# Attention output normalised with features on partitions: values and inverses moved by DMA in place of transposes to tokens and back

## The chip, the cores and the metric

The kernel runs on 1 core of one Trainium2 chip. The metric is the device time in microseconds (us) of one execution. The median of 3 runs of the kernel before is 506.68 us (506.01 to 507.4).

## What is computed

Eight samples of 512 tokens and 256 features go through an attention layer with 16 heads of 16 features, whose output is quantised to int8 and multiplied by a quantised matrix. Cut to what matters here:

```python
q, k, v = heads(x @ wq.T * q_dc), heads(x @ wk.T * k_dc), heads(v_flat)
attn = softmax(einsum('bhqd,bhkd->bhqk', q, k) * scale)
out = einsum('bhqk,bhkd->bhqd', attn, v).transpose(0, 2, 1, 3).reshape(B, S, H)
y = einsum('bsh,oh->bso', out, w_weight) * w_dc[:, None, :] + skip
lhs_scale = max(abs(y), axis=2) / 127        # per token; rhs_scale per column of rhs
return x + int_dot(round(y / lhs_scale), round(rhs / rhs_scale)) * lhs_scale * rhs_scale
```

The softmax is left undivided until after the product with the values: the sum of the exponentials comes out of the same matmul as the values (a column of ones beside them), and its inverse is multiplied in later. That later place is what changes.

## The kernel before

**Steps and rounds.** After a prologue the kernel runs steps t = 0 to 7. Step t does the attention of sample t in 16 rounds, and beside it part A of sample t+1 (load x, modulate, normalise, q, k, v: `has_a`) and part Z of sample t-1 (from the saved attention output to the result: `has_z`). Steps 1 to 6 are three turns of a hardware loop with two steps each, so t = 3 and t = 5 begin with a jump back. Step 7 has no part A, and part Z of sample 7 follows after the last step, by code of its own.

**A round.** Round r is a group of four heads (r // 4) and a tile of 128 keys (r % 4). On PE it is four matmuls for the scores (L933), eight small ones for the values of round r-1 (L946, into `o_acc`, where each head has 32 partitions: 16 of values, then the sum), and then the fill of that round, if it has one. ACT takes the exponentials of the scores in two pieces (L479) and after each fourth round saves `o_acc` into `o_t[:, g, :]` (`save_o`, L465). The last group of sample t-1 is saved in round 0 of step t. Scores of round r+1 need the exponentials of round r, through two buffers.

**Fills.** Part Z of sample t-1 in PE's rounds: `to_natural` (rounds 1 and 2, four times four transposes, from features on partitions to tokens on partitions), `to_features` (round 3, eight transposes back), `projected` with w (rounds 5 and 6, L1078), the transposes of the quantised rows and the integer product (rounds 14 and 15). Part A: `x_transposed` (round 4), then q, k, the skip matrix, and v (rounds 7 to 13, L969, L978, L990). PE runs its program in this order, so a fill that has to wait holds up the scores behind it.

**DVE** does in a step with both parts, in this order: `modulate` and `measure` of x, `z_normalise` (for each 128 tokens the reciprocal of the sums, L742, and the product, L743), `normalise_x` (which waits for a power taken by POOL, L385), `z_features` (two copies from PSUM, L750), two `split`s of the transposed x (L519 to L521), `z_quantise`, and then part A.

**DMA.** SP's queue carries nearly all transfers, issued in program order: after the six transfers to `k_stack` that end a step (L310) it loads x, the style row and three more rows for the next sample (L249, L250, L253), then x once more for the residual (L289), then the 24 transfers of q and k parts.

PSUM tiles for fills come from three banks of `work` in turn; `work_freed` and `work_ready` count them.

Of the kernel before, what the change touches and what calls it, by code (L numbers as in the profile page):

```python
# [19 lines left out]
F32 = mybir.dt.float32  # L20
# [7 lines left out]
P = 128  # L28
# [30 lines left out]
def adaln_ffn_kernel(nc, x, cond, wq, wk, wv, ww, wu, rhs, out):  # L59
# [12 lines left out]
    SETUP_USES, ROW_USES, RHS_USES, A_USES, Z_USES = 7, 2, 3, 12, 12  # L72
# [5 lines left out]
    no_shift_dram = nc.dram_tensor("no_shift_dram", (3, NH, S), BF16).ap()  # L78
    rows_dram = nc.dram_tensor("rows_dram", (B, 3, H), F32).ap()

    ctx = ExitStack()
    with ctx:
# [54 lines left out]
        shift_rest = sb("shift_rest", [NH, S])  # L137
# [17 lines left out]
        inv_den = sb("inv_den", [P, KT, NH])  # L155
        o_nat = sb("o_nat", [P, KT, H])
# [36 lines left out]
        st_ready, exp_done, pv_done, o_saved = sem("st_ready"), sem("exp_done"), sem("pv_done"), sem("o_saved")  # L193
        on_ready, ot_ready, yq_ready, yqt_ready = sem("on_ready"), sem("ot_ready"), sem("yq_ready"), sem("yqt_ready")
# [5 lines left out]
        FULL = ([("on", q) for q in range(KT)] + [("ot", i) for i in range(2)] + [("xt", c) for c in range(HC)]  # L200
# [46 lines left out]
        def _(sp):  # L247
# [26 lines left out]

            def step(t, par, has_a, has_z, base, bank, prologue=False):
# [162 lines left out]
        def _(act):  # L438
# [23 lines left out]
            def save_o(t, g):  # L462

                act.wait_ge(pv_done, t * ROUNDS + KT * (g + 1))
                nc.scalar.activation(o_t[:, g, :], o_acc[:, :], ACT.Copy).then_inc(o_saved, 1)  # L465

            def step(t, par, has_a, has_z, base, bank, prologue=False):
# [5 lines left out]
                for r in range(ROUNDS):  # L473
# [7 lines left out]
                    if r % KT == 0 and r > 0:  # L481
                        save_o(t, r // KT - 1)
# [18 lines left out]
        def _(dve):  # L501
# [111 lines left out]
            def step(t, par, has_a, has_z, base, bank, prologue=False):  # L613
# [41 lines left out]
                if has_z:  # L655
                    z_quantise(ready, pz)
# [91 lines left out]
            def z_features(ready):  # L748
                for i in range(2):
                    link(nc.vector.tensor_copy(o_t2[:, :, 2 * i * P:2 * (i + 1) * P],  # L750
                                               ready("ot", i).rearrange("p (c t) -> p c t", c=HC)))
                    dve.sem_inc(ot_ready, 1)
                    dve.sem_inc(work_freed, 1)
# [394 lines left out]
```

## Time and profile before

| | before |
|---|---|
| median of 3 runs | 506.68 us (506.01 to 507.4) |
| span of the profiled execution | 505.8 us |
| PE busy | 469.7 us, 93% |
| DVE busy | 274.6 us, 54% |
| ACT busy | 290.4 us, 57% |
| POOL busy | 117.2 us, 23% |
| mean granted clock of TensorE | 0.953 |
| DMA, SP's queue | 39.75 MB, 46.8% of 16 engines' span |

The profiled execution is read from its first to its last instruction (the span); the median of the runs lies 0.9 us above it. Busy shares are means over a prologue, eight steps and an end that have different limits. A granted clock of 1 is TensorE's upper level (2.4 GHz), 0.5 its lower one (1.2 GHz). Rows of a timeline merge instructions of one line that follow one another: "x8" is eight of them, the second number is how long the eight took together, and brackets hold the idle time of that engine ahead of the row and what ended it.

### The profile page before, as it was taken

What the parts mean: (1) busy time and instruction counts of PE and PEld (TensorE: products, weight loads), DVE (VectorE), ACT (ScalarE), POOL (GpSimd) and SP (SyncE); (2) the same over time, 40 slices, a digit from 0 to 9 for tenths busy, and PEclk for the clock granted to TensorE, in tenths of its full rate; (3) what the DMA queues carried; (4) which work ended last, traced back from release to release, by engine and by line L of the source; (5) the groups of instructions that cost most, each with busy time, mean ns of one, the idle gap of its engine ahead of it and who ended that gap; (6) DMA issues with size and microseconds to landing.
All of it is one profiled execution on the core that took longest, in us unless ns stands there. A gap on an engine that the chain in (4) does not pass through costs nothing.

```text
span 505.8 us, 8873 instructions
## 1 busy us (share of the span) xinstructions
PE 469.7 (93%) x2626; PEld 225.0 (44%) x2626; DVE 274.6 (54%) x653; ACT 290.4 (57%) x333; POOL 117.2 (23%) x123
## 2 busy tenths in 40 slices
PE   5877999999999999699999999789999999999983
PEld 5753245344553545334543445325454444533251
DVE  4875634267536754357445755447544764444055
ACT  4032675665657575366657665456756665577920
POOL 8532113020324022220322223130232214020021
PEclk9587899999999999889999999979999999999997
DMA  6075629620967068720788049620597219520021
GB/s 202 0 164 112 96 49 129 121 84 2 135 98 191 1 87 102 159 80 1 107 101 191 27 60 127 149 92 0 82 108 152 84 35 128 93 84 1 1 85 41
DMA packets 42029, 45.04 MB, mean 89 GB/s; under 512 B 3896, under 2 KB 39992, under 8 KB 41944
## 3 DMA queue, kind: packets, MB, share of 16 engines
q1 hardware_dynamic: 40096, 39.75, 46.8%
q0 software_dynamic: 1040, 3.72, 1.9%
q8 instruction: 32, 0.52, 0.5%
q10 hardware_dynamic: 832, 0.80, 0.5%
q14 instruction: 29, 0.24, 0.2%
HBM read 14.83 MB, written 4.27 MB: 38 GB/s over the span
## 4 chain that ended last, share of the span: by engine, by line
PE 82%; ACT 4%; issue 4%; DVE 4%; DMA 3%; SPq 1%; POOL 1%; POOLq 0%; ACTq 0%; DVEq 0%
PE o_acc L946 22%; PE scores L933 20%; PE work L969 9%; PE work L990 9%; PE work L809 8%; PE work L1078 6%; ACT probs L479 4%; PE work L978 3%; PE work L838 2%; DMA q_stack<-in_L_cond_w_weight_dram 1%; PE work L1092 1%; DMA rows<-in_cond_dram 1%; SPq L310 1%; DMA q_stack<-no_shift_dram 1%; ACT o_t L465 0%
## 5 line engine op out<-in xcount | busy, mean ns | idle before, releaser
L479 ACT ACTIVATE probs<-scores 128x1024 f32<-128x1024 f32 x256 | 248.0, 1024 | 133.4 <-PE scores L933 133.4
L933 PE MATMUL scores<-q_stack,k_stack 99*128 99x512 bf16 x512 | 138.8, 390 | 13.6 <-issue 9.0
L946 PE MATMUL o_acc<-probs,v_aug 128*32 128x512 f32 x1024 | 139.4, 617 | 0.0
L406 POOL TENSOR_TENSOR parts<-rest,parts 128x512 bf16<-128x512 f32 x32 | 40.8, 1276 | 200.1 <-DVE parts L678 200.1
L933 PEld LDWEIGHTS scores<-q_stack,k_stack 99*128 99x128 bf16 x512 | 43.8, 99 | 85.7 <-ACT probs L479 29.4
L990 PE MATMUL work<-vs_w,x_t 128*128 128x512 f32 x192 | 53.4, 423 | 2.7 <-DVEq L668 2.7
L969 PE MATMUL work<-x_t,qk_w 128*128 128x512 f32 x192 | 53.5, 415 | 0.0
L425 POOL TENSOR_TENSOR rest<-rest,x_res 128x512 f32<-128x512 f32 x16 | 20.0, 1270 | 131.0 <-DVEq L793 131.0
L990 PEld LDWEIGHTS work<-vs_w,x_t 128*128 128x128 f32 x192 | 35.8, 197 | 26.9 <-issue 13.6
L946 PEld LDWEIGHTS o_acc<-probs,v_aug 128*32 128x32 f32 x1024 | 20.4, 109 | 55.8 <-issue 54.1
L969 PEld LDWEIGHTS work<-x_t,qk_w 128*128 128x128 f32 x192 | 34.6, 189 | 23.9 <-DVEq L677 11.7
L1078 PE MATMUL work<-w_demod,o_t 128*128 128x256 f32 x128 | 31.5, 390 | 0.0
L1078 PEld LDWEIGHTS work<-w_demod,o_t 128*128 128x128 f32 x128 | 23.1, 190 | 14.3 <-DVEq L646 5.0
L519 DVE TENSOR_SCALAR upper<-work 128x512 int32<-128x512 int32 x24 | 16.5, 689 | 18.9 <-PE work L978 9.9
L627 DVE TENSOR_TENSOR v_aug<-work,rows 128x256 f32<-128x256 f32 x32 | 13.6, 424 | 24.3 <-PE work L990 24.1
L675 DVE SCALAR_TENSOR_TENSOR rest<-work,col_now,parts 128x512 f32<-128x512 f32 x16 | 12.0, 750 | 25.2 <-ACT parts L459 23.2
L776 DVE TENSOR_SCALAR y_qt<-work 128x512 bf16<-128x512 f32 x14 | 9.7, 692 | 27.9 <-PE work L809 25.8
L459 ACT ACTIVATE parts<-work,col_now 128x512 bf16<-128x512 f32 x16 | 11.0, 688 | 23.6 <-PE work L969 23.6
L459 ACT ACTIVATE parts<-work 128x512 bf16<-128x512 f32 x16 | 9.6, 598 | 24.9 <-PE work L969 24.9
L809 PE MATMUL work<-ident,o_nat 128*128 128x128 f32 x128 | 18.6, 282 | 4.0 <-DVE o_nat L771 2.4
L809 PEld LDWEIGHTS work<-ident,o_nat 128*128 128x128 f32 x128 | 13.6, 140 | 17.6 <-issue 5.9
L465 ACT ACTIVATE o_t<-o_acc 128x512 f32<-128x512 f32 x32 | 19.3, 604 | 3.0 <-PE o_acc L946 3.0
(108 smaller groups left out, 430.2 us busy)
## 6 DMA issues: line engine op xcount, KB each, us to landing
q_stack<-parts SPq DMA_DIRECT2D x96, 128.0 KB, 5.2
k_stack<-parts SPq DMA_DIRECT2D x96, 128.0 KB, 5.3
x_sb<-in_x_dram SPq DMA_DIRECT2D x8, 512.0 KB, 5.5
x_res<-in_x_dram SPq DMA_DIRECT2D x8, 512.0 KB, 3.9
out_dram<-rest POOLq DMA_DIRECT2D x7, 512.0 KB, 4.7
rows<-rows_dram SPq DMA_DIRECT2D x8, 384.0 KB, 5.5
rows<-in_cond_dram SPq DMA_DIRECT2D x8, 128.0 KB, 5.4
out_dram<-rest SPq DMA_DIRECT2D x2, 256.0 KB, 2.1
```

Of the source, the lines that this page charges most:

```text
L406: nc.gpsimd.tensor_tensor(parts[:, n, 2, :], rest[:, n, :], parts[:, n, 1, :], ALU.subtract).then_inc(low_ready, 1)
L425: nc.gpsimd.tensor_tensor(res[:, two, :], res[:, two, :], x_res[:, two, :], ALU.add).then_inc(res_added, 1)
L459: nc.scalar.activation(parts[:, n, 0, :], work[:, (bank + use) % NW, :], ACT.Copy, scale=scale).then_inc(hi_ready, 1)
L465: nc.scalar.activation(o_t[:, g, :], o_acc[:, :], ACT.Copy).then_inc(o_saved, 1)
L479: nc.scalar.activation(probs[:, r % 2, pair:pair + 2, :], scores[:, pair:pair + 2, :], ACT.Exp).then_inc(exp_done, 1)
L519: link(nc.vector.tensor_scalar(top.bitcast(I32), value.bitcast(I32), UPPER_BITS, None, ALU.bitwise_and))
L809: return nc.tensor.transpose(dst, src, ident[0:rows, 0:rows])
L933: last = nc.tensor.matmul(scores[:, j, :], k_stack[0:ROWS, par, h, kt * P:(kt + 1) * P], q_stack[0:ROWS, par, h, :], start=True, stop=True)
L946: last = nc.tensor.matmul(o_acc[DV * j:DV * (j + 1), :], v_aug[:, par, kt, 4 * g + j, :], probs[:, r % 2, j, :], start=(kt == 0), stop=(kt ...
L969: last = nc.tensor.matmul(bank, lhs, right, start=(n == 0), stop=(n == len(operands) - 1))
L990: last = nc.tensor.matmul(bank, lhs, right, start=(n == 0), stop=(n == len(operands) - 1))
L1078: last = nc.tensor.matmul(bank[:, k * H:(k + 1) * H], lhs, right, start=(n == 0), stop=(n == len(operands) - 1))
```

## The change

The 24 transposes of `to_natural` and `to_features` and all of `z_normalise` and `z_features` go, for the samples 0 to 6. Instead SP moves, for each of the four groups of heads, the sums (four partitions of `o_t`, into 16 rows of a new tile `den`) and the values (four transfers of 16 partitions each, straight into `o_t2`, which has features on partitions): 20 transfers in a step. DVE takes one reciprocal of `den`, SP stores it to a tensor in DRAM, waits until it is there, and loads it back in two transfers, each sum repeated over the 16 features of its head (`inv_t`, which lies over half of `rest`). DVE then multiplies `o_t2` by `inv_t` in two halves (`z_scale`), and each half releases one `projected`. ACT's first save in a step waits until the values and sums of the sample before are moved. The end of the last sample is as before.

```diff
-    SETUP_USES, ROW_USES, RHS_USES, A_USES, Z_USES = 7, 2, 3, 12, 12
+    SETUP_USES, ROW_USES, RHS_USES, A_USES, Z_USES = 7, 2, 3, 12, 6
+            def attention_out(g):
+
+                sp.dma_start(den[g * 4 * KT:(g + 1) * 4 * KT, :], o_t[D:P:DV, g, :]).then_inc(den_loaded, 16)
+                half_of = (g % 2) * (P // 2)
+                for j in range(4):
+                    sp.dma_start(o_t2[half_of + j * D:half_of + (j + 1) * D, g // 2, :],
+                                 o_t[j * DV:j * DV + D, g, :]).then_inc(val_loaded, 16)
...
                 if has_z:
                     z = t - 1
+                    for g in range(G):
+                        wait(o_saved, z * G + (g + 1))
+                        attention_out(g)
+                    wait(den_ready, z + 1)
+                    sp.dma_start(inv_dram.rearrange("h (k t) -> (h k) t", k=KT), den_inv[:, :]).then_inc(inv_stored, 16)
+                    wait(inv_stored, z * 16 + 16)
+                    for c in range(HC):
+                        sp.dma_start(inv_t[:, c, :], inv_dram[c * HG:(c + 1) * HG, :].unsqueeze(1)
+                                     .broadcast_to([HG, D, S])).then_inc(inv_loaded, 16)
                     wait(res_added, z * 2 + 2)
...
+                if g == 0 and later:
+                    act.wait_ge(val_loaded, t * G * 4 * 16)
+                    act.wait_ge(den_loaded, t * G * 16)
                 nc.scalar.activation(o_t[:, g, :], o_acc[:, :], ACT.Copy).then_inc(o_saved, 1)
...
-                if has_z:
-                    z_normalise(ready)
                 if has_a and not prologue:
                     normalise_x(a)
                 if has_z:
-                    z_features(ready)
+                    z_inverses(t - 1)
                 if has_a:
                     for c in range(HC):
                         split(x_t[:, 0, c, :], x_t[:, 1, c, :], ready("xt", c))
...
                 if has_z:
+                    z_scale(t - 1)
                     z_quantise(ready, pz)
...
+            def z_inverses(z):
+                dve.wait_ge(den_loaded, z * G * 16 + G * 16)
+                nc.vector.reciprocal(den_inv[:, :], den[:, :]).then_inc(den_ready, 1)
+
+            def z_scale(z):
+                dve.wait_ge(val_loaded, z * G * 4 * 16 + G * 4 * 16)
+                dve.wait_ge(inv_loaded, z * HC * 16 + HC * 16)
                 for i in range(2):
...
+                    two = slice(2 * i * P, 2 * (i + 1) * P)
+                    nc.vector.tensor_tensor(o_t2[:, :, two], o_t2[:, :, two], inv_t[:, :, two], ALU.mult
+                                            ).then_inc(ot_ready, 1)
...
-                return {1: lambda: [to_natural(0), to_natural(1)], 2: lambda: [to_natural(2), to_natural(3)],
-                        3: lambda: [to_features(0), to_features(1)], 5: lambda: projected(0), 6: lambda: projected(1),
+                _, _, projected, quantised_transposed, int_product = z_stages(z, pz, claimed)
+                return {5: lambda: projected(0), 6: lambda: projected(1),
```

DVE, in the loop, from the end of `measure` to the start of `z_quantise`; before (`L621` and `L508` rows are register work for the waits; "waits" names the semaphores):

```order
L539 TENSOR_SCALAR var_eps<-mv 128x4 [waits dve_step]
L742 RECIPROCAL inv_den<-work 128x16 [waits work_ready]
L743 TENSOR_TENSOR o_nat<-work,inv_den 128x256 [waits dve_step]
L544 TENSOR_SCALAR x_sb<-x_sb,mv,rstd 128x256 [waits rstd_ready]
L750 COPY o_t<-work 128x2x256 [waits work_ready]
L519 TENSOR_SCALAR upper<-work 128x512 [waits work_ready]
L520 CAST x_t<-upper 128x512 [waits dve_step]
L521 TENSOR_TENSOR x_t<-work,upper 128x512
L759 TENSOR_TENSOR o_nat<-work,skip 128x512 [waits work_ready]
```

And the same place in the changed kernel:

```order
L567 TENSOR_SCALAR var_eps<-mv 128x4 [waits dve_step]
L572 TENSOR_SCALAR x_sb<-x_sb,mv,rstd 128x256 [waits rstd_ready]
L777 RECIPROCAL den_inv<-den 64x128 [waits den_loaded]
L547 TENSOR_SCALAR upper<-work 128x512 [waits work_ready]
L548 CAST x_t<-upper 128x512 [waits dve_step]
L549 TENSOR_TENSOR x_t<-work,upper 128x512
L781 ISA [waits val_loaded]
L784 TENSOR_TENSOR o_t<-o_t,rest 128x2x256 [waits inv_loaded]
L791 TENSOR_TENSOR o_nat<-work,skip 128x512 [waits work_ready]
```

(The tile `o_t2` shows as `o_t` and `inv_t` as `rest`.) The copies that released `projected` stood ahead of the two splits; the products that release it now stand behind them. The reciprocal stands ahead of the splits and waits for a transfer.

SP, in the loop, between the loads for the next sample and the first part of q; before:

```order
L249 DMA x_sb<-in_x_dram 128x4x256
L250 DMA rows<-in_cond_dram 128x256
L253 DMA rows<-rows_dram 128x768
L289 ISA [waits res_added]
L289 DMA x_res<-in_x_dram 128x4x256
L310 DMA q_stack<-parts 16x8x512 [waits hi_ready]
```

And in the changed kernel:

```order
L261 DMA rows<-rows_dram 128x768
L285 DMA den<-o_t 16x1x128 [waits o_saved]
L288 DMA o_t<-o_t 16x512 x4
L308 DMA inv_dram<-den_inv 64x128 [waits den_ready]
L311 DMA rest<-inv_dram 128x1x512 [waits inv_stored]
L311 DMA rest<-inv_dram 128x1x512
L314 ISA [waits res_added]
L314 DMA x_res<-in_x_dram 128x4x256
L335 DMA q_stack<-parts 16x8x512 [waits hi_ready]
```

The pair L285 and L288 stands there four times, once for each group: 20 transfers, and behind them one store and two loads, each with a wait, on the one queue.

## Rows read from the trace of the kernel before

**Rows 1.** The page, part 4: the chain that ended last, by engine.
```profile
PE 82%; ACT 4%; issue 4%; DVE 4%; DMA 3%; SPq 1%; POOL 1%; POOLq 0%; ACTq 0%; DVEq 0%
```

**Rows 2.** Timeline of PE, step t=4: start us, us, engine, line, op.
```profile
271.05 1.03 PE L933 MATMUL scores<-q_stack,k_stack 99*128 99x512 bf16 x4
...
284.08 1.09 PE L809 MATMUL work<-ident,x_sb 128*128 128x128 f32 x8
285.01 1.03 PE L933 MATMUL scores<-q_stack,k_stack 99*128 99x512 bf16 x4
...
286.96 2.00 PE L1078 MATMUL work<-w_demod,o_t 128*128 128x256 f32 x8
```

**Rows 3.** Timeline of PE, step t=7: starts of rounds 7 and 11, none between filled.
```profile
464.94 1.27 PE L933 MATMUL scores<-q_stack,k_stack 99*128 99x512 bf16 x4
...
473.40 1.28 PE L933 MATMUL scores<-q_stack,k_stack 99*128 99x512 bf16 x4
```

**Rows 4.** Timeline of DVE, step t=4.
```profile
281.77 1.38 DVE L544 TENSOR_SCALAR x_sb<-x_sb,mv,rstd 128x256 f32<-128x256 f32 x4 [0.32 <-DVE o_nat L743]
...
285.06 0.69 DVE L519 TENSOR_SCALAR upper<-work 128x512 int32<-128x512 int32 x1 [0.31 <-DVE o_t L750]
...
289.21 0.69 DVE L759 TENSOR_TENSOR o_nat<-work,skip 128x512 f32<-128x512 f32 x1 [0.32 <-PE work L1078]
```

**Rows 5.** Timeline of POOL, step t=4.
```profile
277.78 1.04 POOL L385 TENSOR_TENSOR rstd<-var_eps,half 128x4 f32<-128x4 f32 x1 [1.77 <-DVE var_eps L539]
```

**Rows 6.** Groups by line and form: count, busy us, mean ns.
```profile
L527 DVE TENSOR_TENSOR x_sb<-x_sb,rows 128x1024 f32<-128x1024 f32 x8 | 10.0, 1253 | 19.3 <-DMA rows<-in_cond_dram 11.8 <-issue 7.0 <-DVE skip L629 0.2
...
L742 DVE RECIPROCAL inv_den<-work 128x16 f32<-128x16 f32 x32 | 8.3, 258 | 18.8 <-PE work L809 12.7 <-DVE o_nat L743 6.1
...
L611 DVE RECIPROCAL demod<-demod 128x80 f32<-128x80 f32 x1 | 0.7, 653 | 0.5 <-ACT demod L448 0.5
```

**Rows 7.** Timeline of SP's queue, end of step t=3 and start of t=4.
```profile
263.26 3.87 SPq L310 DMA_DIRECT2D k_stack<-parts  x6
...
269.04 0.34 SPq L253 DMA_DIRECT2D rows<-rows_dram  x1
```

**Rows 8.** Line L310: one issue, ns min/median/max, of SP's queue.
```profile
L310 SPq DMA_DIRECT2D q_stack<-parts x96: 547/588/1457, 29.6 to 425.8; - x96
```

**Rows 9.** Timeline of SP's queue, prologue: a store, and the load that waits for it.
```profile
26.25 0.37 SPq L263 DMA_DIRECT2D rows_dram<-o_nat  x1
28.02 0.37 SPq L253 DMA_DIRECT2D rows<-rows_dram  x1
```

**Rows 10.** Line L289, the load of 512 KB to x_res, last line of the view.
```profile
DMA to landing us min/median/max: 3.4/3.9/6.2
```

**Rows 11.** Line L253, the broadcast load of 384 KB, last line.
```profile
DMA to landing us min/median/max: 4.6/5.5/6.1
```

**Rows 12.** Timeline of PE after two long idle stretches.
```profile
46.99 1.04 PE L933 MATMUL scores<-q_stack,k_stack 99*128 99x512 bf16 x4 [2.45 <-DMA q_stack<-no_shift_dram]
...
214.28 1.89 PE L933 MATMUL scores<-q_stack,k_stack 99*128 99x512 bf16 x4 [4.36 <-issue]
```

**Rows 13.** Windows: PE busy, then granted clock, DMA share and GB/s.
```profile
49.00:50.00 1.00, 1.00 (x3) 0.50 1.09 155
...
211.00:213.00 2.00, 0.00 (x0) 0.80 0.93 314
...
219.00:221.00 2.00, 2.00 (x15) 0.99 0.02 6
```

**Rows 14.** Timeline of SP's queue, step t=1.
```profile
98.77 0.33 SPq L253 DMA_DIRECT2D rows<-rows_dram  x1
```

**Rows 15.** Timeline of PE, step t=1.
```profile
115.63 1.99 PE L1078 MATMUL work<-w_demod,o_t 128*128 128x256 f32 x8
```

**Rows 16.** Timeline of SP's queue, step t=3.
```profile
209.61 0.34 SPq L253 DMA_DIRECT2D rows<-rows_dram  x1
```

**Rows 17.** Timeline of PE, step t=3.
```profile
231.97 1.99 PE L1078 MATMUL work<-w_demod,o_t 128*128 128x256 f32 x8
```

More of the change, by code:

```diff
@@ L78, in adaln_ffn_kernel @@
     no_shift_dram = nc.dram_tensor("no_shift_dram", (3, NH, S), BF16).ap()
+    inv_dram = nc.dram_tensor("inv_dram", (NH, S), F32).ap()
     rows_dram = nc.dram_tensor("rows_dram", (B, 3, H), F32).ap()
@@ L136, in adaln_ffn_kernel @@
         shift = sb("shift", [NH, 3, S], BF16)
-        shift_rest = sb("shift_rest", [NH, S])
+        shift_rest = upper[0:NH, :]
         probs = sb("probs", [P, 2, 4, S])
@@ L155, in adaln_ffn_kernel @@
         inv_den = sb("inv_den", [P, KT, NH])
+        den = sb("den", [NH * KT, P])
+        den_inv = sb("den_inv", [NH * KT, P])
+        inv_t = rest[:, 0:2, :]
         o_nat = sb("o_nat", [P, KT, H])
@@ L193, in adaln_ffn_kernel @@
         st_ready, exp_done, pv_done, o_saved = sem("st_ready"), sem("exp_done"), sem("pv_done"), sem("o_saved")
+        val_loaded, den_loaded, inv_loaded = sem("val_loaded"), sem("den_loaded"), sem("inv_loaded")
+        den_ready, inv_stored = sem("den_ready"), sem("inv_stored")
         on_ready, ot_ready, yq_ready, yqt_ready = sem("on_ready"), sem("ot_ready"), sem("yq_ready"), sem("yqt_ready")
@@ L197, in adaln_ffn_kernel @@
         spare = sem("spare")
-        FULL = ([("on", q) for q in range(KT)] + [("ot", i) for i in range(2)] + [("xt", c) for c in range(HC)]
+        FULL = ([("xt", c) for c in range(HC)]
                 + [("rows", n) for n in range(ROW_USES)] + [("rhs", n) for n in range(RHS_USES)]
@@ L460, in high_part, with save_o @@
                                      scale=scale).then_inc(hi_ready, 1)
-            def save_o(t, g):
+            def save_o(t, g, later=True):
                 act.wait_ge(pv_done, t * ROUNDS + KT * (g + 1))
+                if g == 0 and later:
+                    act.wait_ge(val_loaded, t * G * 4 * 16)
+                    act.wait_ge(den_loaded, t * G * 16)
                 nc.scalar.activation(o_t[:, g, :], o_acc[:, :], ACT.Copy).then_inc(o_saved, 1)
@@ L481, in step @@
                     if r % KT == 0 and r > 0:
-                        save_o(t, r // KT - 1)
+                        save_o(t, r // KT - 1, has_z)
                     if r == 0 and has_z:
@@ L1041, in z_fills @@
             def z_fills(z, pz, claimed):
-                to_natural, to_features, projected, quantised_transposed, int_product = z_stages(z, pz, claimed)
-                return {1: lambda: [to_natural(0), to_natural(1)], 2: lambda: [to_natural(2), to_natural(3)],
-                        3: lambda: [to_features(0), to_features(1)], 5: lambda: projected(0), 6: lambda: projected(1),
+                _, _, projected, quantised_transposed, int_product = z_stages(z, pz, claimed)
+                return {5: lambda: projected(0), 6: lambda: projected(1),
                         14: lambda: [quantised_transposed(0), quantised_transposed(1)],
@@ L1106, in last_claimed @@
                 elif kind == "on":
[L1107 removed]
+                    pe.wait_ge(on_ready, n - NW + 1)
                 return work[:, use % NW, :]
@@ L1120, in _ @@
                 int_product(i)
-DVE_LINKS = 80
+DVE_LINKS = 60
 _INS = ['x', 'cond_2048', 'L0_cond_q_weight', 'L0_cond_k_weight', 'L0_cond_v_weight', 'L0_cond_w_weight',
```

8 lines of the change are left out of this document (1 added, 7 removed).

## The prediction

> **What bounds the kernel now.** I read the chain first: 82% of it is PE [rows 1], so work taken off PE can pay. But the share is a mean over rounds of two kinds, so I read one step of the loop, t=4, in PE's timeline [rows 2]. Round 0 starts at 271.05, the transposes of x (round 4) at 284.08, round 5 at 285.01, and its fill, the first `projected`, at 286.96. I call this last start P0, since everything behind it keeps its distance from it. Four rounds and the scores and values of the fifth take 284.08 - 271.05 = 13.03 us. What they would take without fills is seen in step 7, whose rounds 7 to 10 have none: 473.40 - 464.94 = 8.46 us for four [rows 3]. This is the pace at which PE and ACT feed each other. So removing the fills of rounds 1 to 3 can give about 2.6 us a step: x_transposed would start at 271.05 + 8.46 + 1.96 (scores and values as in round 5, 286.96 - 285.01) = 281.5. Over seven steps that is 18 us, and the question is whether P0 follows.
>
> **P0 does not follow: DVE's order.** In the trace `projected` is released by the copies ahead of the splits. In the new order the product stands behind both splits, and they need the transposed x. The two splits take 289.21 - 285.06 = 4.15 us [rows 4]. The first bank of x is full about half-way through the eight transposes (1.09 us), so the splits run from 281.5 + 0.7 = 282.2 to 286.35. The product has 512 elements per partition from SBUF; L527 does 1,024 in 1.25 us [rows 6], hence 0.65. With 0.1 for the signal, P0 is 287.1: 0.2 us later than before, and PE, which is ready for it at 281.5 + 2.88 = 284.4, stands still for 2.7 us. This floor holds even if every transfer is free. The 2.6 us won ahead are spent waiting. PE's removed time is real, but it is given back three rounds later.
>
> **The transfers, in a step inside a turn (t = 2, 4, 6).** SP's queue is busy with `k_stack` until 267.13 and ends the issue of its next loads at 269.38 [rows 7]. Then come 20 issues in a row. No SP issue of this size from SBUF to SBUF with few rows is in the trace. The nearest are L310's, also SBUF to SBUF: 0.547 us at the shortest, 0.588 in the median [rows 8], and 3.87 us for six, 0.65 each with the queue full [rows 7]. From DRAM or to it one takes 0.34 to 0.37 [rows 7, 9]. I take 0.60 (bounds 0.40 and 0.65). The sixteenth, which carries the last sums, is issued at 269.38 + 15 x 0.60 = 278.4. It lands within 1.8: the store of 24 KB and the load that waits for it start 1.77 us apart [rows 9]. That makes 280.2. DVE's `normalise_x` no longer waits for the four pairs ahead of it but only for POOL's power, which ends at 278.82 [rows 5]; with its 1.38 us [rows 4] DVE is free at 280.3. The reciprocal has 128 elements per partition; 16 take 0.258 us and 80 take 0.653 [rows 6], so by that slope 0.95: 281.25. SP has meanwhile issued the last four value transfers, until 281.4. Its store and wait take 1.77: 283.2. The two broadcast loads carry 512 KB together. The load of 512 KB at L289 lands in 3.9 (3.4 at best) [rows 10]; the broadcast load of 384 KB takes 4.6 at best and 5.5 in the median [rows 11], behind other loads. I take 4.6, since here the queue ahead is empty but there are two of them: 287.8. The product adds 0.65 and the signal 0.1: P0 = 288.55, 1.6 us later than before, and PE waits 4.1 us. The ends: 0.40 an issue, with loads of 3.4, gives 281.25 + 1.77 + 3.4 + 0.75 = 287.2 (the floor, +0.2); 0.65 an issue, with loads of 6.1, gives an SP free at 269.38 + 13.0 = 282.4 and P0 = 291.0 (+4.1).
>
> **The other steps.** At t=1 SP has its rows issued at 99.1 [rows 14]. So 99.1 + 12.0 = 111.1 for the twentieth issue (the reciprocal is done at 110.85), then 1.77 + 4.6 + 0.75 = 118.25 against 115.63 [rows 15]: +2.6 (bounds 0 and +5.1). At t = 3 and 5 the jump back of the loop delays PE but not SP: SP is through at 209.95 [rows 16], the same sum gives loads landed at 209.95 + 12.05 + 1.77 + 4.6 = 228.4. P0 stood at 231.97 [rows 17]. The transposes of x move from 229.1 to 226.5, the splits end at 231.35, P0 is 232.1: the floor rules, +0.2 each. Step 7 has no splits, but its SP queue is as late after `k_stack`; I price it as an inner step, +1.6. Waits alone: 2.6 + 3 x 1.6 + 2 x 0.2 + 1.6 = +9.4 us (floor everywhere +1.4; upper ends 5.1 + 12.3 + 0.4 + 4.1 = +22).
>
> The Trainium skill (DMA: Bandwidth & Descriptors, Issuing engines are not separate DMA queues) says that initiating a DMA is usually small beside the DMA itself. Row and rule differ here: L310's issue is 0.55 us or more [rows 8]. By the rule the sums at t=1 would be there before DVE asks, and that step would cost about 1.3 us less.
>
> **The clock.** The new stalls of PE are 2.7 us (t = 3, 5), about 4 (t = 2, 4, 6, 7) and longer at t=1. What such stalls do is in the trace. After 4.36 us of waiting at the jump the four scores took 1.89 us instead of 1.03 [rows 2, 12]; the granted clock had fallen before 213 and was back at about 219 [rows 13]. After 2.45 us at 46.99 the scores were still fast, and two microseconds on the clock stood at 0.50 [rows 12, 13]. So half clock lasts some 7 us, of which about 2 lie in the stall, and in the other 5 PE loses (1.89 - 1.03)/1.89 = 0.45 of its time: 2.3 us. It falls into the rounds with the largest fills, where PE sets the pace and nothing covers it. Five stalls of about 4 us and more, and one of the two short ones: 6 x 2.3 = +13.8 us.
>
> **Costed at nothing.** ACT's first save now waits for the last value transfer, issued at 281.4 and landed at 283.2; ACT is there at about 282. Behind it stand the exponentials of round 5, and PE's values of round 4 need the save; both are done by 286, while PE waits for P0 until 288.55. Without that cover it would cost 1.2 us a step. DVE's removed work is ahead of the splits and gives DVE nothing it could use, since the splits wait for PE. The x_res load comes later, and its reader, POOL's addition, comes at the step's end. The extra 1.1 MB a step (512 KB of values, 512 KB of broadcast inverses, 64 KB beside them) fall between 270 and 288, behind the x loads and ahead of the parts of q. Banks of `work` come free earlier than before.
>
> **The sum.** 9.4 + 13.8 = 23.2 on a span of 505.8, which lies 0.9 below the median of the runs: 529.9, I say 530 us.
>
> **The rivals.**
> (a) The clock holds. The stalls are there, but split so that the clock does not fall. For it: PE works densely ahead of the stall, unlike at 46.99. Against it: both stretches in [rows 12] were followed by a fall. 505.8 + 0.9 + 9.4 = 516.
> (b) The broadcast loads are slower than I take. They read 8 rows of DRAM, each repeated 16 times. If each runs on half of the engines, the moving part of 3.9 - 1.8 = 2.1 us doubles: +2.1 a step where the transfers are last (t = 1, 2, 4, 6, 7), +10.5 in all, 540. At t = 3 and 5 there are 2.9 us of slack, which cover it. No row here has such an outer count of 8, so the trace neither supports nor excludes it. The Trainium skill speaks for it (DMA: Bandwidth & Descriptors, Why a DMA increments its semaphore by 16 and not by 1): the number of engines is the largest up to 16 that divides the slowest dimensions of both access patterns, which would be 8.
> (c) No change: issues at 0.40, loads at 3.4, and a clock that holds. Every step is at the floor: 506.7 + 1.4 = 508.
> (d) Faster. If rounds 0 to 3 ran at PE's own pace of 1.96 a round instead of 2.115, T would be 0.6 earlier, and P0 0.4 us earlier than before in each step; with transfers at their low ends and no clock fall, 7 x 0.4 = 2.8 us: 504. The full 18 us (488) need the product ahead of the splits or splits that are off the path; the order on DVE speaks against that. The point from which it turns is P0 before 286.96.
>
> **How the numbers follow.** Chances: my forecast (stalls and clock) 0.47, own range 521 to 538; (b) 0.23; (a) 0.15; (c) 0.07, of which 0.06 within 0.3%; (d) 0.08. A measurement of this kernel tells about 0.3% (1.5 us) from no change. Faster 0.08, same 0.06, slower 0.86. The range leaves out (d) and most of (c) below and the upper tail of (b) above, and takes in +22 us of waits with seven clock falls (545): 509 to 545.
>
> **What would show it.** Right: PE rounds 0 to 3 start about 2.1 us apart; PE idles ahead of L1109 (projected) in each step by 2.7 us or more, released by DVE's L784; L784 itself idles on the landing of L311 in t = 1, 2, 4, 6; SP's twenty issues take about 12 us; the granted clock shows 0.5 behind the stalls, and the mean clock falls from 0.953 to below 0.92. Wrong: issues of 0.3 us (then the floor holds in inner steps), L784 idle only behind the splits, a mean clock near 0.95 (then about 516), or DVE waiting for `den` so long that the splits start late (then above 540).

## The result and the profile after

The changed kernel takes 560.12 us (median of 4 runs, 555.54 to 560.98), the kernel before 506.35 us (505.92 to 507.4) on the same chip. The ratio is 1.1035, with a 95% interval of 1.0983 to 1.1086: 53.8 us slower, where +23 was forecast and 545 us was the upper end. The profiled execution has a span of 559.3 us against 505.8, and a mean granted clock of 0.921 against 0.953. Runs over 1.5% above the fastest of their kernel are left out of all comparisons, which touches only two runs of the first kernel with later projections.

The page of the changed kernel: the engines' busy time, the bytes of SP's queue (q1), and the chain that ended last, by engine (compare [rows 1]) and by line of code.

```profile
PE 468.7 (84%) x2458; PEld 214.8 (38%) x2458; DVE 263.5 (47%) x604; ACT 290.4 (52%) x333; POOL 118.3 (21%) x123
...
q1 hardware_dynamic: 46704, 47.56, 46.4%
...
PE 47%; SPq 26%; DMA 11%; DVE 6%; issue 6%; ACT 3%; DVEq 0%; POOLq 0%; POOL 0%; ACTq 0%
SPq L288 13%; PE o_acc L978 11%; PE scores L965 10%; PE work L1001 8%; PE work L1109 7%; DMA rest<-inv_dram 7%; SPq L335 5%; PE work L1022 5%; SPq L285 3%; PE work L1010 2%; DMA inv_dram<-den_inv 2%; ACT probs L507 2%; PE work L870 1%; PE work L841 1%; DMA q_stack<-in_L_cond_w_weight_dram 1%
```

PE was 82% of the chain and is 47%. SP's queue (SPq) has taken a quarter of it, and the largest single line of the chain is L288, the issue of the value transfers. PE's busy time hardly fell (468.7 from 469.7 us) although 168 transposes are gone: the matmuls of `projected` were busy for 44.0 us in place of 31.5 and the scores for 143.6 in place of 138.8, since a part of them ran at half clock. The view of waits (who waited <- for whom: us in all, times, longest) names the new stalls:

```profile
PE work L1109 <- DVE o_t L784: 41.2, 7, 7.4
DVE o_t L784 <- DMA rest<-inv_dram: 35.2, 7, 9.3
DVE den_inv L777 <- DMA den<-o_t: 22.0, 7, 7.5
...
ACT o_t L493 <- DMA o_t<-o_t: 17.5, 6, 5.0
PE o_acc L978 <- ACT o_t L493: 13.8, 5, 3.7
```

Now step t=4. First PE's timeline, which answers to [rows 2]:

```profile
292.89 1.03 PE L965 MATMUL scores<-q_stack,k_stack 99*128 99x512 bf16 x4
...
303.71 1.09 PE L841 MATMUL work<-ident,x_sb 128*128 128x128 f32 x8
...
308.62 1.07 PE L978 MATMUL o_acc<-probs,v_aug 128*32 128x512 f32 x8 [2.95 <-ACT o_t L493]
315.85 3.77 PE L1109 MATMUL work<-w_demod,o_t 128*128 128x256 f32 x8 [6.17 <-DVE o_t L784]
319.42 1.84 PE L965 MATMUL scores<-q_stack,k_stack 99*128 99x512 bf16 x4
```

The transposes of x start 10.82 us after round 0 (13.03 before): the gain of the freed rounds is there. P0 stands 22.96 us after round 0, and stood 15.91 after it. SP's queue in the same step, which answers to [rows 7, 9]:

```profile
292.26 1.06 SPq L285 DMA_DIRECT2D den<-o_t  x1
293.37 2.49 SPq L288 DMA_DIRECT2D o_t<-o_t  x4
...
296.70 3.36 SPq L288 DMA_DIRECT2D o_t<-o_t  x4
...
303.47 0.59 SPq L285 DMA_DIRECT2D den<-o_t  x1
304.10 2.41 SPq L288 DMA_DIRECT2D o_t<-o_t  x4
306.65 0.50 SPq L308 DMA_DIRECT2D inv_dram<-den_inv  x1
308.56 1.35 SPq L311 DMA_DIRECT2D rest<-inv_dram  x2
```

And DVE's, which answers to [rows 4]:

```profile
300.69 1.60 DVE L572 TENSOR_SCALAR x_sb<-x_sb,mv,rstd 128x256 f32<-128x256 f32 x4 [1.17 <-POOL rstd L410]
305.25 0.94 DVE L777 RECIPROCAL den_inv<-den 64x128 f32<-64x128 f32 x1 [2.95 <-DMA den<-o_t]
...
309.19 0.68 DVE L549 TENSOR_TENSOR x_t<-work,upper 128x512 fp32r<-128x512 f32 x1
315.03 1.29 DVE L784 TENSOR_TENSOR o_t<-o_t,rest 128x512 f32<-128x512 f32 x2 [5.15 <-DMA rest<-inv_dram]
```

Read together they give the chain. The fourth transfer of sums is issued at 303.47, because fifteen issues stand ahead of it. It lands, and the reciprocal runs from 305.25 to 306.19. SP is busy with the last four values until 306.51 and then stores. The loads follow at 308.56, and the product at 315.03, long after the splits (end 309.87). At t=3, an odd step, the product waits for the loads too:

```profile
250.80 1.29 DVE L784 TENSOR_TENSOR o_t<-o_t,rest 128x512 f32<-128x512 f32 x2 [2.68 <-DMA rest<-inv_dram]
```

The clock in the stall, by windows (busy us of PE, PEld, DVE, ACT and POOL; the last three are granted clock, DMA share and GB/s):

```profile
308.00:310.00 2.00, 1.07 (x8) 0.16 (x8) 1.72 (x3) 2.00 (x3) 0.00 (x0) 1.00 0.02 5
310.00:312.00 2.00, 0.00 (x0) 0.00 (x0) 0.00 (x0) 0.40 (x1) 0.00 (x0) 0.70 0.51 165
312.00:314.00 2.00, 0.00 (x0) 0.00 (x0) 0.00 (x0) 0.00 (x0) 0.00 (x0) 0.50 1.01 217
...
318.00:320.00 2.00, 2.00 (x6) 1.18 (x6) 0.34 (x1) 0.00 (x0) 0.00 (x0) 0.50 0.00 0
320.00:322.00 2.00, 2.00 (x12) 0.31 (x9) 1.74 (x6) 1.40 (x2) 0.00 (x0) 0.74 0.00 0
```

PE falls to its lower level while it stands still and keeps it behind the stall (by an estimate from the windows' clocks, from 310.8 to 321): the eight matmuls of `projected` take 3.77 us and not 2.00.

The whole difference can be split at P0. From the starts of round 0 and P0 in both timelines, P0 comes later after round 0 by 6.2 (t=1, counted from the span's start), 6.0, 2.3, 7.0, 2.5, 8.3 and 5.7 us (t = 2 to 7): 38.1 us in all. From P0 to the next round 0 (in t=7 to the end) the steps are longer by 2.2, 3.0, 2.2, 2.1, 2.0, 1.8 and 2.2: 15.4 us. Together that is the 53.5 us between the spans. In all seven steps it is the product L784 that releases P0, and the loads L311 that release L784.

### The profile page after: what moved, and what is told of

Read it like the earlier page. It is cut to its first block, busy times and chain, and to the rows that moved or that the text cites. A ratio compares the mean times of both kernels' runs of the same rounds, so it can differ in the third digit from the quotient of the medians.

```text
span 559.3 us, 8531 instructions
## 1 busy us (share of the span) xinstructions
PE 468.7 (84%) x2458; PEld 214.8 (38%) x2458; DVE 263.5 (47%) x604; ACT 290.4 (52%) x333; POOL 118.3 (21%) x123
## 4 chain that ended last, share of the span: by engine, by line
PE 47%; SPq 26%; DMA 11%; DVE 6%; issue 6%; ACT 3%; DVEq 0%; POOLq 0%; POOL 0%; ACTq 0%
SPq L288 13%; PE o_acc L978 11%; PE scores L965 10%; PE work L1001 8%; PE work L1109 7%; DMA rest<-inv_dram 7%; SPq L335 5%; PE work L1022 5%; SPq L285 3%; PE work L1010 2%; DMA inv_dram<-den_inv 2%; ACT probs L507 2%; PE work L870 1%; PE work L841 1%; DMA q_stack<-in_L_cond_w_weight_dram 1%
## 5 line engine op out<-in xcount | busy, mean ns | idle before, releaser
L965 PE MATMUL scores<-q_stack,k_stack 99*128 99x512 bf16 x512 | 143.6, 396 | 14.7 <-issue 8.5
L978 PE MATMUL o_acc<-probs,v_aug 128*32 128x512 f32 x1024 | 139.5, 617 | 13.8 <-ACT o_t L493 13.8
L965 PEld LDWEIGHTS scores<-q_stack,k_stack 99*128 99x128 bf16 x512 | 41.7, 101 | 110.5 <-ACT probs L507 57.6
L1109 PE MATMUL work<-w_demod,o_t 128*128 128x256 f32 x128 | 44.0, 504 | 41.2 <-DVE o_t L784 41.2
L1022 PE MATMUL work<-vs_w,x_t 128*128 128x512 f32 x192 | 52.1, 415 | 2.7 <-DVEq L695 2.7
L1109 PEld LDWEIGHTS work<-w_demod,o_t 128*128 128x128 f32 x128 | 30.7, 251 | 59.0 <-issue 46.3
L493 ACT ACTIVATE o_t<-o_acc 128x512 f32<-128x512 f32 x32 | 19.3, 604 | 21.8 <-DMA o_t<-o_t 17.5
L791 DVE TENSOR_TENSOR o_nat<-work,skip 128x512 f32<-128x512 f32 x16 | 11.1, 691 | 34.2 <-PE work L1109 34.2
L784 DVE TENSOR_TENSOR o_t<-o_t,rest 128x512 f32<-128x512 f32 x14 | 9.1, 688 | 35.2 <-DMA rest<-inv_dram 35.2
L484 ACT ACTIVATE parts<-work 128x512 bf16<-128x512 f32 x16 | 9.6, 598 | 24.2 <-PE work L1001 24.2
```

What stands on the lines that cost most here:

```text
L484: nc.scalar.activation(parts[:, n, 0, :], work[:, (bank + use) % NW, :], ACT.Copy, scale=scale).then_inc(hi_ready, 1)
L965: last = nc.tensor.matmul(scores[:, j, :], k_stack[0:ROWS, par, h, kt * P:(kt + 1) * P], q_stack[0:ROWS, par, h, :], start=True, stop=True)
L978: last = nc.tensor.matmul(o_acc[DV * j:DV * (j + 1), :], v_aug[:, par, kt, 4 * g + j, :], probs[:, r % 2, j, :], start=(kt == 0), stop=(kt ...
L1022: last = nc.tensor.matmul(bank, lhs, right, start=(n == 0), stop=(n == len(operands) - 1))
L1109: last = nc.tensor.matmul(bank[:, k * H:(k + 1) * H], lhs, right, start=(n == 0), stop=(n == len(operands) - 1))
```

## The experiments

Each edits the changed kernel. Ratios are to the kernel before on the same chip, with 95% intervals.

**No inverse.** The reciprocal, the transfers of sums, the store and the loads go, so the division is left out; the product becomes a maximum of `o_t2` with itself, in the same place:

```diff
-                sp.dma_start(den[g * 4 * KT:(g + 1) * 4 * KT, :], o_t[D:P:DV, g, :]).then_inc(den_loaded, 16)
...
-                    sp.dma_start(inv_dram.rearrange("h (k t) -> (h k) t", k=KT), den_inv[:, :]).then_inc(inv_stored, 16)
...
-                    z_inverses(t - 1)
...
-                    nc.vector.tensor_tensor(o_t2[:, :, two], o_t2[:, :, two], inv_t[:, :, two], ALU.mult
+                    nc.vector.tensor_tensor(o_t2[:, :, two], o_t2[:, :, two], o_t2[:, :, two], ALU.max
```

> The changed kernel without its inverse chain: no transfers of sums, no reciprocal, no store to DRAM, no broadcast loads; the product keeps its place behind the splits, with another operand that is there already (the division by the sums is left out). My theory (transfers of the inverse set the start of the first projection, and DVE's order is the next limit): the first projection starts at the floor, about 16.1 us after round 0 (22.96 now, 15.9 before), PE still idles some 2.7 us ahead of it, and the time is 508 to 520 us, by how often the clock falls. Rival (DVE's order is no limit): the projection starts when PE comes to it, 13.4 us after round 0, and the time is about 488.

Measured: 513.3 us, 1.0133 (1.0113 to 1.0153), clock 0.958. PE's timeline in t=4:

```profile
292.57 1.99 PE L1098 MATMUL work<-w_demod,o_t 128*128 128x256 f32 x8 [2.13 <-DVE o_t L773]
```

P0 stands 16.5 us after round 0 in t = 2, 4 and 6 and 17.6 to 18.8 in t = 3 and 5. With nothing but the order on DVE left, PE still waits about 2 us a step, and the kernel is no faster than before. So the floor is real, and of the 54 us about 46 hang on the inverse.

**No inverse, product ahead of the splits.** The same, and `z_scale` moves to where `z_inverses` stood:

```diff
-                    z_inverses(t - 1)
+                    z_scale(t - 1)
...
-                    z_scale(t - 1)
```

> As e1_no_inverse (the division is left out), and the product stands ahead of the two splits on DVE. My theory: it is then bound only by the landing of the 16 value transfers, some 12 us after round 0, PE idles 0 to 1 us ahead of the first projection, the clock stays up, and the saving of the transposes shows: 490 to 496 us. Rival (the value transfers alone are as slow as the whole): above 505.

Measured: 494.36 us, 0.9757 (0.9734 to 0.9779). P0 comes 14.5 us after round 0 in t = 2 and 4. Moving the product by one place on DVE is worth 19 us. The freed rounds pay when nothing stands between them and P0, but only 12 us, and in a kernel that leaves out the division.

**The order of the broadcast load.** The 16 copies become the outermost dimension. The bytes are the same, but the features get the inverse of another head:

```diff
-                        sp.dma_start(inv_t[:, c, :], inv_dram[c * HG:(c + 1) * HG, :].unsqueeze(1)
-                                     .broadcast_to([HG, D, S])).then_inc(inv_loaded, 16)
+                        sp.dma_start(inv_t[:, c, :], inv_dram[c * HG:(c + 1) * HG, :].unsqueeze(0)
+                                     .broadcast_to([D, HG, S])).then_inc(inv_loaded, 16)
```

> The changed kernel with the two broadcast loads read in another order: 16 copies outermost, 8 heads inside, in place of 8 heads outermost (same bytes, same 2 KB pieces; features get the inverse of another head, so part of the result is not the reference's). If the loads run on half of the engines because of the outer count of 8: they land in about 4.3 us instead of 6.4, the first projection is 2.1 us earlier in each of seven steps, and the time falls by about 15 us to 545. If the 6.4 us are the price of a broadcast from DRAM behind other transfers: no change, 560.

Measured: 547.36 us, 1.0839 (1.0768 to 1.0909). SP's queue and DVE in t=4:

```profile
302.10 1.21 SPq L311 DMA_DIRECT2D rest<-inv_dram  x2
...
306.78 1.29 DVE L784 TENSOR_TENSOR o_t<-o_t,rest 128x512 f32<-128x512 f32 x2 [3.36 <-DMA rest<-inv_dram]
```

From the issue of the loads to the product it takes 4.7 us, and 6.5 in the changed kernel; over the steps t = 2 to 7 it is 4.3 to 4.9 us, and 5.4 to 7.7 in the changed kernel. The windows show why. In the changed kernel, before the load of x_res joins:

```profile
311.00:311.50 0.50, 0.00 (x0) 0.00 (x0) 0.00 (x0) 0.00 (x0) 0.00 (x0) 0.50 0.51 150
311.50:312.00 0.50, 0.00 (x0) 0.00 (x0) 0.00 (x0) 0.00 (x0) 0.00 (x0) 0.50 0.52 143
```

And with the copies outermost:

```profile
304.00:304.50 0.50, 0.00 (x0) 0.00 (x0) 0.00 (x0) 0.00 (x0) 0.00 (x0) 0.50 0.83 324
304.50:305.00 0.50, 0.00 (x0) 0.00 (x0) 0.00 (x0) 0.00 (x0) 0.00 (x0) 0.50 1.10 303
```

The load with 8 outer rows keeps a share of 0.51 to 0.52 of the 16 engines busy at about 150 GB/s, the one with 16 outer copies 0.83 and more at over 300. This is rival (b), and it is real. The rule of the Trainium skill that I weighed for it (DMA: Bandwidth & Descriptors, Why a DMA increments its semaphore by 16 and not by 1) gives 8 engines and 16 for these two shapes. The trace agrees, with a share of 0.51 against 0.83 and more. The run is 12.8 us faster than the changed kernel by the medians and 10 us by the ratios; some 15 us were expected.

**Work for PE in the stall.** Dummy matmuls into the claimed bank ahead of the wait for the product, 44 of them, and in a second kernel 20:

```diff
+                    if i == 0 and pad:
+                        for _ in range(pad):
+                            nc.tensor.matmul(bank[:, 0:P], ones[:, :], ident[:, :], start=True, stop=True)
```

> The changed kernel with 44 matmuls that feed nothing ahead of PE's wait for the first projection, about 5 us of work inside the stall. My theory (the stall costs the clock too, about 2.5 us a step): the first projection starts at the same distance from round 0, its eight matmuls take 2.0 us instead of 3.8, the granted clock stays near 1 and the time falls by 12 to 18 us, to 542 to 548. Rival (the clock falls for other reasons, or costs nothing, since PE has slack): 560, or above it if the padding delays something.

> As e4_keep_clock with 20 matmuls in place of 44. There each took 0.23 us (two passes of 0.115), so the padding lasted 10 us, longer than the stall; 20 take 4.6 us, less than the stall of 5 to 7. My theory (the stall costs the clock as well): first projection at the same distance from round 0 as in the changed kernel, its eight matmuls in 2.0 us and not 3.8, mean clock 0.95 or more, 542 to 548 us. Rival (the clock is not what the stall costs): 558 to 562.

Measured: with 44, 579.65 us, 1.1429 (1.1385 to 1.1473), a miss. PE's timeline at t=3:

```profile
251.56 10.09 PE L1104 MATMUL work<-ident,ones 128*128 128x128 f32 x88
```

The trace counts two instructions for each f32 matmul, and the padding took 10.1 us, longer than the stall that it should fill. With 20: 546.72 us, 1.0809 (1.075 to 1.0868), clock 0.945. Its PE timeline at t=4:

```profile
302.39 1.07 PE L978 MATMUL o_acc<-probs,v_aug 128*32 128x512 f32 x8 [2.85 <-ACT o_t L493]
303.39 6.34 PE L1104 MATMUL work<-ident,ones 128*128 128x128 f32 x40
309.57 1.89 PE L1112 MATMUL work<-w_demod,o_t 128*128 128x256 f32 x8
```

P0 stands 22.8 us after round 0, as late as without the padding, but `projected` takes 1.89 us. The 40 instructions took 6.34 us, 0.16 each, where those of the longer padding took 0.115: the clock had fallen here too, and came back while the padding ran. The windows of this run at t=4 show it (granted clock third from the end):

```profile
303.00:304.00 1.00, 1.00 (x11) 0.61 (x4) 0.66 (x2) 1.00 (x2) 0.00 (x0) 0.69 0.17 35
305.00:306.00 1.00, 1.00 (x7) 1.00 (x6) 0.00 (x0) 0.00 (x0) 0.00 (x0) 0.50 0.61 195
307.00:308.00 1.00, 1.00 (x11) 1.00 (x10) 0.50 (x1) 0.00 (x0) 0.00 (x0) 1.00 1.02 331
```

So at t=4 (and at t=2) the half clock fell on matmuls that feed nothing, behind PE's wait for ACT of 2.85 us; at t=3 the clock stood at 1.00 throughout. Behind P0, the steps t = 1 to 6 are together 0.4 us longer than before, and 13.2 us longer in the changed kernel, while P0 comes as late as there (0.6 us earlier over all seven steps together). So the surplus behind P0 is the clock, and 13.4 us of the median (11 by the ratios) is its price.

**Sums first.** SP issues three transfers of sums ahead of the values and the store ahead of the last four:

```diff
-                    for g in range(G):
+                    for g in range(G - 1):
                         wait(o_saved, z * G + (g + 1))
-                        attention_out(g)
+                        sums_out(g)
+                    attention_out(0)
+                    wait(o_saved, z * G + G)
+                    sums_out(G - 1)
+                    attention_out(1)
+                    attention_out(2)
...
+                    attention_out(3)
```

> The changed kernel with SP's issues in another order: the four transfers of sums ahead of most values, the store after the values of three groups, the last four values while the store is under way. If SP's queue of twenty issues of 0.7 us sets when the inverse starts: the store goes out 3 us earlier, the first projection comes about 19.7 us after round 0 in place of 23.0, and the time is 535 to 543 us. Rival (the loads or DVE's place set it, and the order does not matter): 555 to 560.

Measured: 557.9 us, 1.1006 (1.0939 to 1.1074): a miss, no clear change. SP's queue, first at t=3, then at t=4:

```profile
227.57 2.54 SPq L289 DMA_DIRECT2D o_t<-o_t  x4
233.90 0.59 SPq L284 DMA_DIRECT2D den<-o_t  x1
234.53 5.60 SPq L289 DMA_DIRECT2D o_t<-o_t  x8
...
303.68 0.50 SPq L314 DMA_DIRECT2D inv_dram<-den_inv  x1
304.23 2.49 SPq L289 DMA_DIRECT2D o_t<-o_t  x4
306.92 1.35 SPq L318 DMA_DIRECT2D rest<-inv_dram  x2
```

At t=4, counted from round 0, the store comes 2.7 us earlier, but the four value issues behind it end only 3.0 us after it was issued (a store and the load behind it were 1.9 apart): the loads gain 1.4 us and P0 1.5. At t=3 SP stands still from 230.1 to 233.9, since the save of the last group only comes in round 0, which the jump back delays; P0 is 1.5 us later there. Over the whole kernel this order, with the number of issues as it was, made no clear difference.

**Projections later.** `projected` moves from rounds 5 and 6 to rounds 8 and 9, and DVE's product behind its share of k; the inverse lies in the other half of `rest`, and its loads wait for POOL's store out of it. The second kernel has sums first and a semaphore for each group too; the third is the second with the product one place earlier on DVE:

```diff
+                    late = [fills.pop(5), fills.pop(6)] if has_z else None
...
+                        fills[8] = lambda: [k0(), late[0]()]
+                        fills[9] = lambda: [late[1](), q1()]
```

> The changed kernel, transfers untouched, with both projections (and DVE's product and quantising) moved behind q and k of the first group: rounds 8 and 9 in place of 5 and 6; the inverse lies in the other half of rest. My theory (the chain of transfers is only too long for round 5, about 23 us after round 0; round 8 ends its own work at about 22): PE's stall at the projection falls under 2 us, ACT's wait for the values stays at some 3 us a step and is now the largest loss, and the time is 500 to 515 us. Rival (the transfers cost by contention with the parts of q and k, or by the clock): above 530.

> e6 and e7 together, and a semaphore for each group of heads, so that ACT's first save waits for the first group's values alone. My theory: no stall of PE over 1 us is left in a step but the jump of the loop, rounds 0 to 6 run at 2.1 us, the clock stays near 0.96 to 1, and the time is 486 to 494 us, faster than both kernels. Rival (what was taken off PE comes back in any order, in the rounds of part A, where DVE now has the quantising between the parts of q and k): 500 to 508.

> e8_late_sums_groups with DVE's product by the inverse ahead of the second part of A (k of the first group) and no longer behind it. In e8 PE stood still for 4 us at the projection while DVE did that part, although the inverse had landed. My theory: P0 follows the matmuls of k without a stall over 1 us, the clock stays up outside the loop's jumps, and the time is 495 to 508 us. Rival (something else than DVE's place holds the projection, or the parts of q and k are late in turn): above 525.

Measured: 554.45 us, the median of the two runs that count (560.09 over all four), 1.0952 (1.0857 to 1.1048); 543.88 us, 1.0742 (1.0687 to 1.0796); 511.99 us, 1.0131 (1.0055 to 1.0208). The first two are misses by 40 and 50 us, and the third lies 4 us above what was expected. DVE's timeline of the second at t=4:

```profile
303.43 0.75 DVE L714 SCALAR_TENSOR_TENSOR rest<-work,col_now,parts 128x512 f32<-128x512 f32 x1 [5.17 <-ACT parts L493]
...
306.66 0.69 DVE L711 TENSOR_TENSOR rest<-work,parts 128x512 f32<-128x512 f32 x1 [1.56 <-ACT parts L493]
...
308.18 2.24 DVE L798 TENSOR_TENSOR o_t<-o_t,rest 128x512 f32<-128x512 f32 x2
```

The product does not wait for a DMA any more (no bracket): it waits for its turn behind work that waits for ACT, and PE's `projected` waits 3.96 us for it, in each of the steps t = 1 to 6 and in the first kernel too. I had moved PE's side and left the same mistake on DVE. In the third kernel this is mended, in PE's timeline at t=4:

```profile
290.35 1.99 PE L1129 MATMUL work<-w_demod,o_t 128*128 128x256 f32 x8 [0.81 <-DVE o_t L799]
...
321.84 0.61 PE L1143 MATMUL work<-rhs_q,y_qt 128*128 128x256 bf16 x4 [1.72 <-DVEq L827]
```

In t = 1 to 6 the stall is down to 0.8 us and the half clock is gone; of the 54 us about 46 come back, 31 of them by this one place on DVE. It is still 1.3% slower than the kernel before. Two remainders are seen: the integer product now waits for DVE's queue (5.5 us in three waits), and in t=7 the projection still starts late and at half clock (3.78 us). The first comes with the semaphores: the three kernels that have one for each group show this wait (4.9 to 6.4 us), and none of the others does. How the rest divides was not measured; the two products together also take 2.24 us in the second kernel, and 1.29 in the changed one.

**A semaphore for each group.** ACT's save waits for its own group's transfers, not for all:

```diff
-                if g == 0 and later:
-                    act.wait_ge(val_loaded, t * G * 4 * 16)
-                    act.wait_ge(den_loaded, t * G * 16)
+                if later:
+                    act.wait_ge(val_loaded[g], t * 4 * 16)
+                    act.wait_ge(den_loaded[g], t * 16)
```

> The changed kernel with only the semaphores split by group of heads, so that ACT's save in round 4 waits for the first group's transfers and no longer for all twenty. My theory, as in the prediction (that wait is covered by the longer wait for the inverse): PE's stall of some 3 us ahead of its values in round 5 goes, its stall ahead of the projection grows by as much, and the time stays, 555 to 562 us. Rival (the wait of ACT costs on its own): 6 steps x 3 us less, about 541.

Measured: 559.59 us, 1.1055 (1.0971 to 1.114). ACT's wait (17.5 us) and PE's for ACT (13.8) are gone from the view, and PE's wait for the product has grown by 4.8 us, from 41.2:

```profile
PE work L1112 <- DVE o_t L787: 46.0, 7, 10.1
...
PE work L1126 <- DVEq L815: 4.9, 3, 1.9
```

The time is the same, but not all of PE's 13.8 us went into the wait for the product. P0 stands 7.3 us earlier after round 0 over all steps together, and the stretches behind P0 are 6.4 us longer, in t = 2, 4 and 6 above all, where PE waits for DVE's queue ahead of the integer product. Why the extra semaphores bring that wait was not examined. So the run bounds the price of ACT's wait at some 7 us, and does not show it to be nothing.

**The values left out**, alone, and with the other order of the load. With the values goes ACT's wait for them:

```diff
-                for j in range(4):
-                    sp.dma_start(o_t2[half_of + j * D:half_of + (j + 1) * D, g // 2, :],
-                                 o_t[j * DV:j * DV + D, g, :]).then_inc(val_loaded, 16)
```

> This kernel is the changed one without its sixteen value transfers a step; the tile of the values is set to zero once and the values stay left out. The four transfers of sums, the reciprocal, the store, the two loads and the product stand where they stood. Theory (SP's queue of issues delays the inverse): the fourth transfer of sums no longer stands behind twelve value transfers, so in an even step the reciprocal waits for normalise_x alone (done about 9.4 us after the start of round 0), then 0.95 + 1.9 for the store and its wait and 6.5 from the issue of the loads to the product: the first projected starts 18.5 to 19.5 us after round 0 in even steps instead of 22.96 at t=4 (15.9 before), and the save of ACT waits for nothing. The time is 532 to 545 us, and DVE's wait for the inverse falls from 35 to 13 to 20 us. Rival (the issues lie beside other work, and only the round trip of the inverse counts): less than 5 us come back, 555 to 560.

> This kernel is the one without value transfers, and its two loads of the inverse have the 16 copies as their outermost dimension, as in the run with that order, so the features get the inverses of another head; the values are left out. Theory (both delays lie in one chain and add up): loads to product 4.7 us instead of 6.5, the first projected 16.8 to 17.6 us after round 0 in even steps, which is close to the floor set by the splits (16.5); DVE's wait for the inverse below 8 us in all, the clock falls in fewer steps, time 515 to 530 us. Rival (with the values gone the load's order is hidden anyway): no more than 3 us below the kernel without value transfers.

Measured: 538.6 us, 1.0648 (1.0567 to 1.0729), and 524.16 us, 1.0348 (1.0273 to 1.0423). SP's queue of the first at t=4:

```profile
281.36 3.80 SPq L285 DMA_DIRECT2D den<-o_t  x4
292.37 0.50 SPq L304 DMA_DIRECT2D inv_dram<-den_inv  x1
```

The sums are out long before DVE asks. P0 stands 18.5 to 20.2 us after round 0 in even steps (21.9 to 24.2 in the changed kernel; 18.5 to 19.5 expected), in the second kernel 17.7 to 18.0, which is 0.1 to 0.4 over what was expected. Both medians lie in their ranges, but DVE's wait for the inverse fell from 35.2 only to 22.9 us (13 to 20 expected) and to 14.3 (below 8 expected). By the ratios some 20 us hang on the sixteen value transfers (21.5 by the medians). How much of that is ACT's wait was not separated. With them gone the order of the load is worth 15 us (14.4 by the medians): the two delays lie in one chain and add up.

## Why the prediction was off

The direction and the place (PE ahead of `projected`, released by L784) were as forecast, and in the even steps the mechanism too (L784 waits for L311). In the odd steps DVE's order was forecast to rule, and the chain of transfers ruled there as well. The size was wrong: P0 came 38.1 us later in all, and the forecast gave it 9.4, with 22 as the upper end. What failed is the length of the chain of transfers, in two of its terms: the price of an issue on SP and the time of the broadcast loads. Step by step:

- **The freed rounds.** Forecast: x's transposes 10.4 us after round 0. Measured 10.82 at t=4. Right.
- **The floor by DVE's order.** Forecast 0.2 us over the old P0. Without the inverse P0 is 0.6 us over it in t=2 and t=4. Right as a floor, but it rules nowhere in the changed kernel.
- **The issues on SP: the term that was mis-sized most.** I took 0.60 us an issue, bounds 0.40 and 0.65, from [rows 7, 8]. Fifteen issues took 11.2 us at t=4 (0.75 each, from 292.26 to 303.47) and 12.7 at t=3 (0.84 each); all twenty took 14.25 at t=4, where 12.0 was forecast. A single value issue is 0.52 at best and 0.59 in the median, but some take up to 1.78. At t=4 the long ones are in the first two groups (1.06 for the first issue, 3.36 for four of the second group, 2.41 for four of the last). [rows 7] had shown 0.65 for L310 in a full queue, and I used this as an upper bound, not as the likely value; even the bound was too low. SP also came to them 0.8 us later after round 0 than before. Together the store is issued 3.4 us later against round 0 than forecast.
- **The reciprocal and the round trip of the store.** Forecast 0.95 and 1.77; measured 0.94 and 1.91. Right.
- **The broadcast loads.** Forecast 4.6 us, measured 6.47 at t=4 (5.4 to 7.7 over the steps), and 4.7 with the copies outermost (4.3 to 4.9). My term was right for 16 engines, and the case was rival (b), whose price was right (2.1 against 1.8) and whose chance was 0.23. I had called the rows silent on it, and the Trainium skill's rule, which the prediction cites, was the only evidence there was. It deserved more.
- **The odd steps.** Forecast: the floor, +0.2, because SP is not held up by the jump. Measured +2.3 and +2.5, and at t=3 too the product waits for the loads. SP did start 4.4 us ahead of round 0 at t=3, as forecast (4.3), but its fifteen issues took 12.7 us in place of 9.0 and the loads 5.7 in place of 4.6. The slack of 2.9 us that I had counted was gone.
- **t=4 as a sum.** 17.5 (forecast P0 after round 0) + 3.4 (issues and start) + 0.14 (store) + 1.87 (loads) + 0.07 = 23.0, against 22.96 measured.
- **The clock.** Forecast 13.8 us, as six falls of 2.3; 15.4 us lie behind P0, as seven of 2.2 in the mean, and filling the stalls gives back 13.4. Right within the noise. At t=4 the half clock lasted some 10 us and not 7, but 5 of them lay in the stall and 5 behind it, and the price hangs on those behind, which were 5 in the forecast too. Rival (a) is out.
- **Costed at nothing.** ACT's wait for the values is 17.5 us long in all, and PE's for ACT 13.8. Taken away by a semaphore for each group, it leaves the time as it was. But that is a balance of two changes of 6 to 7 us, so that it costs nothing is not shown. In the kernels with later projections the second, which differs from the first in the groups' semaphores and the sums first, is 11 us faster. Which of the two gave it was not separated.

The Trainium skill's sentence that initiating a DMA is usually small beside the DMA (DMA: Bandwidth & Descriptors, Issuing engines are not separate DMA queues) fits a single value transfer, whose issue takes 0.59 us and which lands 2.0 us after it, in the median. It does not carry over to a row of them: twenty hold the queue for 14.25 us at t=4, and without sixteen of them the kernel is 20 us faster.

What stays open: why single issues on SP stretch to 1.78 us (loads of x were issued just ahead of them, but no run took those away; at t=7, which has none, the fifteen issues took 10.2 us, the least of all steps, and still more than 9.0), and what else than the wait ahead of the integer product makes up the 6 us by which the best complete version (the third with later projections) is behind the kernel before. No version with the whole computation is faster than before.

## What to carry to other kernels

Many small transfers on one queue are a serial program: count the issues, take the price of one from the stretch where the queue is full, and put the one that somebody waits for first only if nothing behind it delays its answer. Before work is taken off the busiest engine, look at what its next wait is tied to on the other engines; here one place on DVE's list was worth 19 us, and the same mistake came back when the projections were moved, where the place was worth 31. For a broadcast load look at the order of its dimensions: here 8 rows outermost cost 1.8 us a load pair against 16 copies outermost, at t=4, for the same bytes.

## What the runs showed that was not expected

- The load with 8 outer rows ran at a DMA share of 0.51 and about 150 GB/s, the same 512 KB with 16 outer copies at over 300 GB/s. It was a rival; that the share would show it so plainly was not.
- An issue of a transfer of 32 KB cost SP 0.52 to 1.78 us.
- Stalls of 5 to 7 us cost PE, beside themselves, some 2.2 us each through the clock. Dummy matmuls in the stall (6.34 us of them at t=4) did not keep the clock up there, but had it back at 1.00 before P0, with P0 no earlier.
- A semaphore for each group of heads brought three waits of PE for DVE's queue, 4.9 us in all, in another part of the step.
